# New ranks for the order of work after the main part of layer 0: end of layer 0, layers 1, 2 and 3

## What is computed

```python
x = x + _L0_attn_ref(xn, ...) + _L0_ffn_ref(xn, ...)    # linear attention blocks; transformer block with grouped experts
xn = _layernorm(x, axis=-1)
x = x + _L1_attn_ref(xn, ...) + _L1_ffn_ref(xn, ...)    # gated slot attention; 8 experts
xn = _layernorm(x, axis=-1)
x = x + _L2_attn_ref(xn, ...) + _L2_ffn_ref(xn, ...)    # state space layer; 14 experts, 2 for each token
xn = _layernorm(x, axis=-1)
x = x + _L3_attn_ref(xn, ...) + _L3_ffn_ref(xn, ...)    # causal attention; feed-forward quantised to FP4

# layer 2, attention branch, for every sequence; 16 states for each of 256 inner channels
dt = softplus(dt_raw @ W_dt + b_dt)
def step(h, inp):
    dA = exp(dt_t[..., None] * A)
    h = dA * h + dt_t[..., None] * B_t[:, None, :] * x_t[..., None]
    y = einsum('bds,bs->bd', h, C_t)
y = (ys + D_param * xc) * silu(z); out = y @ W_out

# layer 2, feed-forward branch
top2_p, top2_i = top_k(softmax(x @ gate_w.T), 2); w = top2_p / sum(top2_p)
hh = gelu(x @ w1[e] + b1[e]); out_e = hh @ w2[e] + b2[e]
result = clip(x + w0 * out_e0 + w1 * out_e1, -100, 100)
```

## Time and profile before

| | us |
|---|---|
| median of three executions | 1672.18 |
| the profiled execution, own time | 1671.64 |
| its span in the trace | 1669.9 |
| main part of layer 0 | 0 to 785 |
| end of layer 0 | 785 to about 958 |
| layer 1 | to about 1160 |
| layer 2 | to about 1528 |
| layer 3 | to 1669.9 |

### The profile page before, as it was taken

How to read it: one execution, slowest core, us unless ns; L and a number is a source line. 1 busy time by engine, 2 the same in 40 slices (tenths; PEclk the granted TensorE clock), 3 DMA queues, 4 the chain that set the end, 5 groups by cost and what they waited for, 6 DMA issues and landing times. The chain is left out here.

```text
span 1669.9 us, 20205 instructions
## 1 busy us (share of the span) xinstructions
PE 1493.9 (89%) x7054; PEld 652.9 (39%) x7054; DVE 1262.7 (76%) x1760; ACT 1163.8 (70%) x1619; POOL 298.1 (18%) x267
## 2 busy tenths in 40 slices
PE   7899999999999999998999899999986678678998
PEld 3222222223322222222434356664432555243675
DVE  5988888878888888882334437874599899996997
ACT  6689999999999998986523458434555577334663
POOL 1111111111111111111000000000289100682000
PEclk9999999999999999999999989999998899888999
DMA  6200101010100100001152021112444687530000
GB/s 196 67 13 7 26 13 26 13 26 13 26 13 7 26 7 13 7 1 31 39 95 82 19 74 40 46 33 68 141 159 136 209 259 227 175 129 3 1 1 26
DMA packets 66718, 104.19 MB, mean 62 GB/s; under 512 B 9015, under 2 KB 32534, under 8 KB 66596
## 3 DMA queue, kind: packets, MB, share of 16 engines
q1 hardware_dynamic: 55354, 65.15, 14.1%
q10 hardware_dynamic: 9216, 33.56, 6.1%
q0 software_dynamic: 2048, 4.20, 0.9%
HBM read 86.92 MB, written 15.87 MB: 62 GB/s over the span
## 5 line engine op out<-in xcount | busy, mean ns | idle before, releaser
L1138 DVE TENSOR_REDUCE best<-banks 128x2 f32<-128x1024 f32 x256 | 305.6, 1220 | 52.6 <-PE banks L902 50.9
L1034 ACT ACTIVATE weights<-banks 128x1024 f32<-128x1024 f32 x256 | 249.2, 1043 | 5.6 <-PE banks L927 5.3
L3056 PE MATMUL banks<-l_st,ident 128*128 128x512 f32 x256 | 134.3, 670 | 42.1 <-DVE l_st L3367 41.9
L1170 POOL PARTITION_BROADCAST sq_all<-mq x64 | 65.0, 1015 | 516.6 <-ACT mq L976 512.4
L943 PE MATMUL banks<-weights,values 128*32 128x512 f32 x1024 | 137.3, 607 | 4.3 <-ACT mixed L1041 1.9
L111 PE MATMUL banks<-q,wf 128*128 128x512 f32 x256 | 120.5, 605 | 2.9 <-DVE best L1138 1.6
L111 PE MATMUL banks<-hid,wf 128*128 128x512 f32 x256 | 118.0, 603 | 0.2
L902 PE MATMUL banks<-ks,qs 48*128 48x512 bf16 x512 | 91.7, 387 | 15.2 <-ACT weights L1034 9.5
L927 PE MATMUL banks<-qs,ks 49*128 49x512 bf16 x512 | 90.2, 386 | 15.6 <-ACT weights L1034 6.5
L3056 PEld LDWEIGHTS banks<-l_st,ident 128*128 128x128 f32 x256 | 51.8, 214 | 112.6 <-DVE l_st L3367 59.0
L2955 POOL DMA_INDIRECT slots<-l_rows,l_blocks_index x32 | 86.5, 2703 | 42.0 <-ACT l_rows L3173 32.5
(11 more groups left out here) (459 smaller groups left out, 3027.6 us busy)
## 6 DMA issues: line engine op xcount, KB each, us to landing
l_bs<-xd_dram ACTq DMA_DIRECT2D x32, 512.0 KB
l_c_rows<-xd_dram ACTq DMA_DIRECT2D x32, 512.0 KB
end_cs<-comb SPq DMA_DIRECT2D x32, 256.0 KB, 3.7
l_cs<-comb SPq DMA_DIRECT2D x32, 256.0 KB, 3.5
l_weights<-in_F_w SPq DMA_DIRECT2D x30, 257.0 KB, 4.4
wf<-in_L_f SPq DMA_DIRECT2D x16, 256.0 KB, 2.7
l_rows<-in_F_w SPq DMA_DIRECT2D x15, 257.0 KB, 4.7
qs<-q_dram SPq DMA_DIRECT2D x16, 192.0 KB, 3.5
```

Source lines behind the costliest of these rows:

```text
L1034: nc.scalar.activation(weights[p % BUFS][:, slot, :, :], banks.of("weigh", m, i), ACT.Exp, scale=scale).then_inc(weighed, 1)
L1138: nc.vector.tensor_reduce(heads[:, :, slot, qt, c], banks.of("search", m, i), AX.X, ALU.max).then_inc(search_read, 1)
L3056: last = nc.tensor.matmul(y[d][:, c:c + BANK], core.ident[:, :], st[n % RING][:, c:c + BANK], start=False, stop=(s == NS - 1), skip_group_ ...
```

## The change

The tables PLAN_END, PLAN_HALF, PLAN_TILE, PLAN_EXPERT, PLAN_2, PLAN_CAUSAL, PLAN_PIECE, PLAN_FP4 and PLAN_LAST_NORM get new numbers. Before they were fractional times, or in layer 2 ranks counted for each engine apart; now they are whole ranks, in layer 2 counted from 0 to 825 over all engines together. PLAN_TILE lists all 16 tiles now, where before it gave one period's times and a period of 6.6 was added. The main part of layer 0 keeps its table. Nothing of the computation changes; the table loads of ScalarE's functions, which follow its order, are 152 where there were 143. The core of the diff:

```diff
-PLAN_TILE_PERIOD = 6.6
...
     def tile(name, n):
-        return PLAN_TILE[name][n // GT] + n % GT * PLAN_TILE_PERIOD
+        return PLAN_TILE[name][n]
...
 PLAN_2 = {
...
-    "scatter": (2, 3, 4, 5, 6, 7, 8, 9, 10, 11, 12, 13, 14, 15, 16, 17, 18, 19, 20, 21, 22, 23, 24, 25, 26, 27, 28, 29, 30, 31, 32, 33,),
...
+    "scatter": (129, 133, 137, 140, 144, 147, 150, 153, 157, 159, 164, 167, 169, 172, 176, 177, 187, 191, 193, 197, 201, 205, 209, 212, 229, 233,
+        235, 239, 242, 245, 249, 252),
```

More of the change, by code:

```diff
@@ L1612 @@
[L1612 to L1618, removed]
+    "out": (0, 10, 19, 37),
+    "res": (28, 29, 31, 45),
+    "centre0": (30, 32, 53, 54),
+    "square0": (33, 35, 55, 57),
+    "var0": (34, 36, 56, 58),
+    "root0": (38, 39, 59, 61),
+    "scaled0": (40, 42, 62, 66),
+    "affine0": (41, 44, 63, 67),
+    "b2": (99, 102, 180, 205),
+    "res2": (147, 184, 206, 247),
@@ L1619 @@
+    "add": (104, 107, 112, 117, 122, 125, 138, 143, 146, 149, 170, 174, 177, 179, 181, 182, 191, 196, 199, 200, 201, 202, 203, 204, 216, 221, 224,
+        240, 242, 243, 244, 245),
+    "logits": (69,),
+    "exps": (74,),
+    "turn": (81,),
+    "store": (84,),
+    "stored": (90,),
+    "comb": (90,),
+    "route": (71, 75, 83),
 }
@@ new lines @@
+    "eg": ((123, 149, 150, 154), (184, 201, 210, 211)),
+    "weights": ((118, 140, 145, 160), (185, 202, 206, 209)),
+    "ends": ((99,), (152,)),
+    "decay_ends": ((126,), (168,)),
+    "add": ((171, 182), (213, 216)),
+    "copy_add": ((179, 189), (217, 219)),
+    "states": ((191, 192, 194, 196), (222, 223, 228, 257)),
+    "scale": ((197,), (259,)),
+    "Skt": ((207,), (333,)),
+    "copy_Skt": ((214,), (335,)),
+    "square": ((384,), (521,)),
+    "mean": ((480,), (523,)),
+    "log": ((489,), (525,)),
@@ L1957 @@
+    "b2": (94, 167, 319, 477),
+    "join": (165, 313, 455, 535),
+    "comb": (84, 86, 98, 170),
+    "route": (50, 65, 74, 78),
+    "logits": (46,),
+    "count": (72,),
+    "turn": (76,),
+    "choice": (58,),
+    "store": (79,),
+    "stored": (84,),
 }
@@ new lines @@
+    "x": (27, 36, 52, 55, 93, 100, 106, 117),
+    "z": (25, 139, 216, 221, 224, 240, 587, 589),
+    "xd": (60, 63, 145, 155),
+    "dt": (65, 68, 75, 80, 186, 189, 192, 195),
+    "out": (530, 551, 822, 823),
+    "logits": (50,),
+    "ranks": (58,),
+    "turn": (72,),
+    "rows": (122, 130, 160, 213),
+    "turned": (271, 272, 275, 314, 329, 365, 396, 449, 464, 474, 529, 557),
+    "hidden": (279, 281, 283, 292, 346, 350, 360, 374, 381, 400, 412, 426, 428, 451, 463, 470, 504, 506, 509, 512, 552, 554, 565),
@@ new lines @@
+    "made": (317, 332, 361, 394, 407, 432, 466, 479, 516, 538, 567, 583),
+    "sum": (664, 705, 733, 755),
+    "st": (67, 168),
+    "b_row": (91, 103, 116, 118, 152, 173, 217, 248, 267, 287, 296, 310, 344, 382, 388, 418, 446, 461, 503, 523, 550, 580, 586, 631, 643, 673, 688,
+        721, 757, 773, 780, 792),
+    "c_row": (101, 121, 143, 180, 183, 200, 232, 263, 297, 302, 316, 337, 372, 391, 421, 439, 491, 510, 540, 556, 574, 606, 625, 658, 676, 693, 727,
+        753, 772, 783, 799, 803),
@@ L2687 @@
+    "gate": (505, 511, 820, 821),
+    "join": (539, 562, 824, 825),
+    "route": (53, 57),
+    "number": (61,),
+    "copy_turn": (76,),
+    "weigh": (79,),
 }
@@ L3456 @@
[L3456 to L3459 removed]
+    "xb": (76, 125),
+    "copy_xb": (81, 135),
+    "gT": (79,),
+    "copy_gT": (87,),
+    "dT": (262,),
+    "copy_dT": (264,),
+    "gate": (106, 107, 119, 131, 150, 228, 231, 279),
+    "up": (102, 121, 144, 188, 220, 267, 277, 286),
+    "silu": (109, 113, 123, 140, 158, 232, 235, 283),
```

373 lines of the change are left out of this document (148 added, 225 removed).

## The result

Slower. Four executions of the changed kernel took 1713.4 to 1726.35 us, median 1724.82; the kernel before, on the same chip in this and the earlier runs, has a median of 1672.95. The ratio of undisturbed executions is 1.0272 (95% interval 1.0236 to 1.0309), the quotient of the two medians 1.031. Times the 1672.2 of before, the ratio gives 1717.7, 45 us more; 1700 (+28) was forecast, within 1677 to 1720. Three of the four executions took longer than the 1720 at which the range ends: the forecast holds by the ratio, and narrowly.

A forecast was written before the change was run, and what follows sets the result against it. It took VectorE's chain of scan turns to bound layer 2, and TensorE the other stages. From 1671.6 us, +29 for layer 2, -2 for the end of layer 0, 0 for layer 1 and +2 for layer 3 gave 1700, range 1677 to 1720.

The forecast's parts named there:

- the two stops: Layer 2: VectorE stands 30 us for the experts' slots, then 14 us at the sums that wait for gathers.
- rival B: Layer 2: scatters don't speed up while VectorE stands; they end at 1316, restart 1329, +47, about 1717 us; chance 0.15.
- The bound: Layer 2 is a chain of 64 scan turns on VectorE; whatever makes it wait lengthens the kernel one for one.
- The scatters and the first stop: Layer 2: scatters start near 1218.7, end at 1298; VectorE stops at 1281, restarts at 1311.3, 30 us where 7.8 were.
- Rival A: Layer 2: the slow scatters do not occur, they end at 1285; +15 or +8, 1680 to 1686 us; chance 0.14.
- the rule of the Trainium skill: Layer 2: a stopped VectorE would not speed up scatters; they end at 1316, the sum some 17 us more.
- From the restart to the first gather: Layer 2: about 122 us from VectorE's restart to the first gather, as before; gathers start at 1433.
- The sums: Layer 2: earlier sums hold VectorE to the gathers' pace, 14 us of waits; sum.3 free near 1505, end 1543.
- The tail of layer 2: join.0 and join.1 (1.3 us) leave it, but a 0.9 wait and the last gate stand there: 0.
- The other stages: End of layer 0 -2, layer 1 0, layer 3 +2; together 0, with 5 us either way.
- C: Layer 2: GpSimd's trains short enough, under 62 us, so no stops occur; faster, 1657 us; chance 0.09.
- D: Stops real but mild: TensorE-bound stages gain 5 to 8 us, scatters end near 1290; 1680 to 1688 us; chance 0.10.

The follow-up runs named there:

- row_loads_first: The changed kernel with four loads of B and C rows on ScalarE's queue moved ahead of waits for gathers; measured 1.0321 of the kernel before.
- joins_last: The changed kernel with GpSimd's clips and joins put behind all 32 gathers, as before; measured 1.0258 of the kernel before.

## Why the prediction was right, and where it was not

The direction and the two stops were right, with their mechanism; the size was not. By the ratio the loss is 45 us where 28 were forecast. The time, 1717.7, is above even the forecast's own 1691 to 1711, and the number that it met is the 1717 of rival B, whose mechanism did not occur. So that 1717.7 lies in the range is owed to the room left for B, and is luck. Within the scans the terms miss like this: standing 33.2, 12.5 and 22.5 us against 30, 0 and 14 forecast, 24.2 more; work 298.9 against 295.4; first product at 1201.5 instead of 1205.2. Together 24 us, from the forecast 1544.6 to 1568.6.

*The bound.* Right: in layer 2 the loss is VectorE's standing, one for one (54.8 of the 60.7 us by which the scans got longer; the rest is work that moved into the cuts).

*The scatters and the first stop.* Right in mechanism and size: start 1218.7 forecast, 1217.98 measured; end 1298 and 1297.86; restart 1311.3 and 1310.75; stop 30 and 32.60, and c_row.8 held VectorE up for 0.90 us. That they agree to under 1 us is luck: 1298 was a choice between bounds of 1285 and 1316, and the stage began 2.7 us earlier than in before, which these times did not reckon with. That the train speeds up in the stop, which I rested on a single gather (before has a second of 0.95 us, at 1446.94), holds for 15 scatters in a row. Rival A is out, since 13 scatters of the changed kernel took 2.8 to 6.4 us; so are rival B's mechanism and the sum that goes by the rule of the Trainium skill, which had no speed-up in the stop.

*From the restart to the first gather.* The step that failed: "Both come to about 122 us". It was 134.0. VectorE's work in it was 121.55 us, which fits the 122; its standing, which the sum put at nothing, was 12.5 (4.32 and 3.82 for adds behind experts' pieces, 2.87 for rows of B), where before had 2.5. The check was no check: the old 120 us held 24 turns, the new stretch 26, and two turns more are 8.9 us. The adds are spread differently among the experts there, and I counted none of these places.

*The sums.* Right in mechanism, too small in size: 14 us of stops forecast, 22.5 measured. I took the sums as the only thing that waits; on ScalarE the rows of C for turns 54 and 55 stand behind scale.24 to 31, and the 8.15 us for them I had looked for only at the first stop. row_loads_first shows that moving these loads alone gains nothing. The last sum was done near 1524.6, not 1505: 11.8 of it because the gathers started late, 2.4 because they took 73.4 us, the rest in landing and scales. From there it took 44 us and not 38, since VectorE had just stood for rows and was not four turns ahead. The count of VectorE's work was 295.4, and it was 298.9.

*GpSimd's queue.* clip.0, join_experts.0, clip.1 and join_experts.1 had moved in among the gathers, and the prediction did not say so. joins_last puts the price at under 3 us.

*The tail of layer 2.* Taken as 0; from the last product with C to the first matmul of layer 3 it was 14.55 us before and 11.65 now.

*The other stages.* -2 + 0 forecast for the first two, -2.7 measured, but as a difference of two errors: the last matmul of the end of layer 0 is 11.9 us earlier, where I had seen only the 3.39 us wait and not the 4.1 us for cen_all next to it, and layer 1 is 9.2 us longer, where I had put 0, with bubbles of 2 in it. Layer 3: +2 and +2.5.

*Rivals.* C (faster, if the trains were short) is out: the trains were 79.9 and 73.4 us. D too. Two of their numbers were off: B's own sum, 1671.6 + 47 and the offset, makes 1719 and not 1717, and VectorE idled 13.4 us in the scans of before, not the 14.6 that C names.

What stays open is how the loss in layer 2 divides. The early sums are enough for 2.4% in before, but taking them back, the experts' places back, or both, leaves at least 2.1% in the changed kernel.

## What to carry to other kernels

Count what an engine does between two cuts and how long it stands there: when work is constant, the sum of its stops is the loss, and moving one wait only pays if no other wait takes its place, which here one mostly did. Where a slow train of transfers (here 32 of them, twice) feeds an engine that works in order, place its consumers by the train's measured pace, and remember that the consumers' own work can set that pace. A stage whose time hardly changed may hold a gain and a loss of the same size: put in its tables one at a time; here that gave a kernel 0.8% faster than before out of a change that made it 2.7% slower.

## What the runs showed of the hardware

An indirect transfer issued by GpSimd takes 0.95 to 0.96 us beside an idle VectorE (15 scatters of the changed kernel, 1279.23 to 1296.90). Beside working products and scans, which all have two inputs in SBUF, it ends 0.76 to 0.84 us after the end of a VectorE instruction, in 31 of 32 scatters of before: the one that starts at 1211.00 ends at 1212.83, the scan beside it at about 1212.06. Where it starts beside VectorE's work decides how long it takes. Two of the eight slow scatters of before started within 0.1 us of the start of a scan and lasted through it, 2.97 and 2.96 us; in the changed kernel six gathers did, 2.96 to 2.97 us each. Five ran past two to four products and ended after the scan behind them, such as the one from 1233.13 to 1240.68, the longest; the eighth ended after a product behind which VectorE stood 0.44 us:

```profile
1233.13 7.55 POOL L2955 DMA_INDIRECT slots<-l_rows,l_blocks_index  x1 [0.30 <-issue]
```

The Trainium skill, "SBUF — State Buffer", section "Who interferes with whom", says that a VectorE instruction with two SBUF inputs contends with a GpSimd instruction that reads SBUF. The traces agree, if issuing an indirect transfer counts as one that reads. They don't agree with what the same section reports of a probe and explains by an inference, that tensor_tensor did not stall transfers that GpSimd issued: the scatter of before at 1219.77 ran beside three tensor_tensor alone and took 2.01 us, and beside products and scans together they take up to 7.55, eight times their 0.95.
